# Combining five partial score maxima into the exponential's bias: from one VectorE instruction to three dependent GpSimd instructions

## The reference, cut to what matters

```python
attn = jnp.einsum('bhqd,bhkd->bhqk', q, k)          # q, k: integers of -127..127 times a step
attn = jax.nn.softmax(attn.astype(jnp.float32), axis=-1)
attn = _fq_unsigned(attn, axis=-1)                  # row maximum / 255 is the step; round to 0..255
out = jnp.einsum('bhqk,bhkd->bhqd', attn, v)
```

## Time and profile before

| | us |
|---|---|
| Three executions | 6569.11, 6581.19, 6591.67 |
| Median | 6581.19 |
| Profiled execution | 6572.37 |
| Its span, first to last instruction | 6570.9 |
| Cross-attention's unit stage, within the span | about 433 to 5330 |
| Busy within the span: VectorE | 5686.5 (87%) |
| ScalarE | 4572.5 (70%) |
| TensorE matmuls | 4523.2 (69%) |
| GpSimd | 4505.6 (69%) |

### The profile page before, as it was taken

The page is one execution under the profiler, slowest core; times in us unless marked ns, Lnnn a source line. Parts: engine busy times, 40 slices in busy tenths (PEclk is TensorE's granted clock), DMA queues, the critical chain, the costliest instruction groups (busy, mean ns, idle before and its releaser), DMA issues. The chain is left out here.

```text
span 6570.9 us, 141175 instructions
## 1 busy us (share of the span) xinstructions
PE 4523.2 (69%) x48970; PEld 2144.1 (33%) x49686; DVE 5686.5 (87%) x7938; ACT 4572.5 (70%) x4949; POOL 4505.6 (69%) x3196
## 2 busy tenths in 40 slices
PE   6736666666666666666666666666666645769999
PEld 3412222222222222222222222222222233454555
DVE  7579999999999999999999999999999955873222
ACT  3328888888888888888888888888888843331111
POOL 1238888888888888888888888888888833420000
PEclk9769999999999999999999999999999977989999
DMA  3137677677677677677777777766766740010000
GB/s 118 51 76 140 139 140 143 138 140 142 139 141 142 135 144 141 139 142 139 141 139 141 141 137 140 144 137 140 142 139 140 138 105 4 0 35 4 6 6 10
DMA packets 2231911, 735.21 MB, mean 112 GB/s; under 512 B 2175779, under 2 KB 2209412, under 8 KB 2225573
## 3 DMA queue, kind: packets, MB, share of 16 engines
q1 hardware_dynamic: 2196261, 576.08, 42.2%
q0 software_dynamic: 35456, 157.33, 13.2%
HBM read 168.97 MB, written 27.26 MB: 30 GB/s over the span
## 5 line engine op out<-in xcount | busy, mean ns | idle before, releaser
L803 DVE TENSOR_SCALAR_CACHE_REDUCE scores<-ring,step 128x2048 f32<-128x2048 f32 (+2 forms) x2560 | 4780.3, 1918 | 44.4 <-PE ring L730 28.0
L882 ACT ACTIVATE n_op<-scores,bias 128x2048 uint8<-128x2048 f32 x2048 | 4075.1, 1992 | 493.5 <-DVE m_rest L810 493.5
L678 POOL CAST nT<-pairs 128x2048 f16<-128x2048 uint8 x2048 | 3791.3, 1890 | 561.0 <-DMA pairs<-n_op 536.7
L730 PE MATMUL ring<-x_all,q_op 128*128 128x512 bf16 x7746 | 2153.7, 386 | 863.2 <-DVE scores L803 773.1
L730 PEld LDWEIGHTS ring<-x_all,q_op 128*128 128x128 bf16 x8192 | 683.0, 98 | 2021.1 <-DVE scores L803 1330.1
L727 PE MATMUL ring<-x_all,q_op 128*128 128x512 bf16 x1793 | 572.9, 390 | 808.0 <-DVE scores L803 780.3
L742 PE MATMUL pO<-nT,v_op 128*32 128x128 f16 x32768 | 660.1, 224 | 20.6 <-POOL nT L678 20.6
L742 PEld LDWEIGHTS pO<-nT,v_op 128*32 128x32 f16 x32768 | 478.5, 98 | 467.1 <-issue 359.2
L727 PEld LDWEIGHTS ring<-x_all,q_op 128*128 128x128 bf16 x2048 | 116.7, 97 | 1035.6 <-DVE scores L803 1028.3
L882 ACT ACTIVATION_READ_ACCUMULATOR n_op<-scores,bias 128x1 f32 x2048 | 384.7, 188 | 0.0
L1637 DVE TENSOR_TENSOR h_up<-h_gate,pUp 128x512 f32<-128x512 f32 x112 | 76.9, 687 | 298.2 <-ACT h_gate L1626 298.2
(11 more groups left out here) (194 smaller groups left out, 3293.2 us busy)
## 6 DMA issues: line engine op xcount, KB each, us to landing
x_all<-keys_transposed POOLq DMA_DIRECT2D x128, 768.0 KB, 8.4
v_st<-value_integers POOLq DMA_DIRECT2D x128, 256.0 KB, 3.5
pairs<-n_op SPq DMA_TRANSPOSE x2048, 2.8
keys_transposed<-kT_s POOLq DMA_DIRECT2D x32, 384.0 KB, 3.5
x_all<-in_x SPq DMA_DIRECT2D x2, 4096.0 KB, 14.9
cT<-in_ctx_T SPq DMA_DIRECT2D x32, 256.0 KB, 3.0
q_op<-queries_transposed POOLq DMA_DIRECT2D x384, 16.0 KB, 8.4
value_integers<-v_int SPq DMA_DIRECT2D x1, 4096.0 KB, 12.2
```

Source lines behind the costliest of these rows:

```text
L678: nc.gpsimd.tensor_copy(nT[par][:, j * EK:(j + 1) * EK, :].rearrange("p (a c) b -> p a c b", c=2), src).then_inc(s_un, 1)
L730: mm = nc.tensor.matmul(slot(t, j)[:, n * BANK:(n + 1) * BANK], q_op[b][:, t * P:(t + 1) * P], k_op[b][:, at + n * BANK:at + (n + 1) * BAN ...
L803: nc.vector.tensor_scalar(score[t % 2][:, at:at + width * BANK], slot(t, j)[:, 0:width * BANK], step[b][:, t:t + 1], None, ALU.mult, ALU.m ...
L882: nc.scalar.activation(n_op[par][:, j * EW:(j + 1) * EW], score[par][:, j * EW:(j + 1) * EW], ACT.Exp, bias=bias[par][:], scale=-1.0, accu ...
```

## The change

`make_bias` leaves VectorE's list and enters GpSimd's. There the five columns of `m_part` are combined in three instructions on one column each: min of columns 0, 1, 2; min of that with columns 3, 4; then ln 255 is added. The second and the third wait for the one before them on a new semaphore, `maxima_combined`. The bias of unit u+1 is made behind cast 0 of unit u (in unit 3 of a head group that is ahead of `keys`), and it waits for the last score copy, D4, of unit u+1. The bias of the first unit is made ahead of the loop.

```diff
@@ -533,7 +533,7 @@
         PAIRS = KT // 2
         HEADS = NG * H
         PE_STEPS = "M2 M3 AV0 M4 AV1 N0 N1 FOLD".split()
-        DVE_STEPS = "D0 BIAS FIN DEN D1 INV D2 D3 D4".split()
+        DVE_STEPS = "D0 FIN DEN D1 INV D2 D3 D4".split()
         ACT_STEPS = "E0 E1 OC E2 E3".split()
 
         assert NM % RING == 1 and all(sum(w) * BANK == NK for w in WIDTH)
@@ -569,6 +569,7 @@
         s_vo = sem("head_values_staged", xs)
         s_m = sem("scores_ready", xs)
         s_mu = sem("scores_copied", xs)
+        s_mr = sem("maxima_combined", xs)
         s_b = sem("bias_ready", xs)
         s_eu = sem("exp_done", xs)
         s_n = [[sem(f"turned{p}{j}", xs) for j in range(NE)] for p in range(2)]
@@ -678,10 +679,26 @@
                     nc.gpsimd.tensor_copy(nT[par][:, j * EK:(j + 1) * EK, :].rearrange("p (a c) b -> p a c b", c=2), src
                                           ).then_inc(s_un, 1)
 
+                def make_bias(u, par):
+                    pool.wait_ge(s_mu, scored(u, NM - 1))
+                    pool.sem_inc(s_turn, 1)
+                    m = m_part[par]
+                    nc.gpsimd.tensor_scalar(m_rest[par][:, 0:1], m[:, 0:1], m[:, 1:2], m[:, 2:3], ALU.min,
+                                            ALU.min).then_inc(s_mr, 1)
+                    pool.wait_ge(s_mr, u * 2 + 1)
+                    pool.sem_inc(s_turn, 1)
+                    nc.gpsimd.tensor_scalar(m_rest[par][:, 1:2], m_rest[par][:, 0:1], m[:, 3:4], m[:, 4:5], ALU.min,
+                                            ALU.min).then_inc(s_mr, 1)
+                    pool.wait_ge(s_mr, u * 2 + 2)
+                    pool.sem_inc(s_turn, 1)
+                    nc.gpsimd.tensor_scalar(bias[par][:], m_rest[par][:, 1:2], LN255, None, ALU.add).then_inc(s_b, 1)
+
                 def head(g, h, i):
                     for t in range(TG):
                         u = i * TG + t
                         unpack(u, t, 0)
+                        if exists(u + 1):
+                            make_bias(u + 1, (t + 1) % 2)
                         if t == 3 and exists(u + 2 * TG):
                             keys(g + (h + 2) // H, (h + 2) % H, i + 2)
                         unpack(u, t, 1)
@@ -708,6 +725,7 @@
                 for b in range(2):
                     pool.wait_ge(s_vo, b + 1)
                     load_values(2 + b, b)
+                make_bias(0, 0)
                 for h in range(H):
                     head(0, h, h)
                 with pool.Fori(1, NG - 1) as g:
@@ -804,12 +822,6 @@
                                             step[b][:, t:t + 1], None, ALU.mult, ALU.min,
                                             accum_out=m_part[t % 2][:, j:j + 1]).then_inc(s_mu, 1)
 
-                def make_bias(u, par):
-
-                    dve.wait_ge(s_mu, scored(u, NM - 1))
-                    nc.vector.tensor_scalar(m_rest[par][:], m_part[par][:], LN255, None, ALU.add, ALU.min,
-                                            accum_out=bias[par][:]).then_inc(s_b, 1)
-
                 def denominators(i, b):
                     dve.wait_ge(s_eu, exped(i * TG + TG - 1, NE - 1))
                     ge(dve, s_rd, i)
@@ -838,8 +850,6 @@
                                 if x == "D0" and t1 == 0:
                                     dve.wait_ge(s_st, i + 2)
                                 copy_scores(u + 1, int(x[1]), b, t1)
-                        elif x == "BIAS":
-                            make_bias(u, par)
                         elif t == 1 and exists(i - 1) and x != "FIN":
                             if x == "DEN":
                                 denominators(i - 1, 1 - hp)
```

## The result

The kernel after takes 7090.6 us in the median of four runs (7069.1 to 7092.2), against 6575.9 us for the kernel before beside it: ratio 1.078, 95% interval 1.076 to 1.080. The time of 7030 us was forecast, in a range of 6720 to 7400. The execution that the profiler recorded is the fastest of the four, 7069.1 us.

What follows compares the result with a forecast made beforehand. VectorE bounds before at 38.1 us per head group; then GpSimd at 33.7 + 4 x 0.96 + wait 4.1 = 41.6. The extra 3.5 x 128 = 450 us takes 6572 to 7022, plus 9 for the median: 7030, range 6720 to 7400.

Steps and rivals of the forecast that it cites:

- a wait of 2: GpSimd's wait for quarters behind the keys' load: 2 us instead of about 4 would show the prediction wrong.
- Its sign of over 3 us of idle time per head group at the score copies: VectorE's score copies: over 3 us idle per head group, put down to exponentials or TensorE, would show the prediction right.
- I take 0.18, by the COPY, which is nearest in size: Price of one new GpSimd instruction: 0.18 us, from a 4-element COPY; bounds 0.14 to 1.22.
- The wait of 0.23: GpSimd's new instructions: each wait for its own previous result costs 0.23 us, two per unit.
- b: GpSimd time added per unit by the three bias instructions: 2 x 0.18 + 2 x 0.23 + 0.14 = 0.96 us.
- So the transfer is issued 0.2 ahead of K: Unit 3's last quarter goes out 0.2 us before GpSimd issues the keys' load (8.3 against 8.5 after the bias).
- the long wait: GpSimd's wait per head group for a quarter sharing DMA engines with the keys' load: 4.1 us, used in the sum.
- up to 0.19 x 128 = 24 us more: VectorE ahead of FIN: extra saving of up to 24 us, if FIN's waits are taken during D0.
- 512 x 0.08 = 41: VectorE's saving from losing BIAS: 0.08 us each, 41 us in all, if VectorE stays the bound.
- Short wait: Rival: keys issued late enough for unit 3's last quarter to slip through; wait 2.1, round 39.6, time 6770; 16%.
- dearer instructions: Rival: GpSimd instructions with column operands have a fixed cost of 0.5 us; round 43.6 to 45.6, 7290 to 7540; 11%.
- GpSimd takes it in: Rival: GpSimd's round stays under 37.8 us, VectorE bounds and gives 41 to 65 us: 6516 to 6540; 9%.

Runs made afterwards that it cites:

- The chain beside the unchanged kernel: Kernel before, bias still on VectorE, plus the same three dependent GpSimd instructions at the same place on spare data, nobody waiting for them: 6827.9 us, ratio 1.038.
- the run without the dependence: Kernel after with three GpSimd instructions that read no result of each other, their two waits gone, bias constant: 7015.5 us, ratio 1.069.
- The run without a bias: Kernel before without any bias instruction; exponentials wait for their unit's last score copy and take a constant bias: 6522.9 us, ratio 0.992.
- the keys issued later: Kernel after with the keys' step in unit 3 moved behind cast 3 instead of behind the bias: 7134.7 us, ratio 1.086.
- five links: Kernel after with five dependent GpSimd instructions in place of three, two more copies of the second, same result: 7619.2 us, ratio 1.161.

## Why the prediction was right, and where two of its terms were not

**The bound.** Right: GpSimd's round of work plus its own wait took the lead over VectorE. Rounds foretold and measured: 41.6 and 42.0 us. The chain beside the unchanged kernel shows the work alone is enough for half of the loss. That the time came within 60 us is luck in part: two terms of the sum were wrong by over 200 us each, in opposite directions, and one of the prediction's own signs of being wrong, a wait of 2, did appear. Its sign of over 3 us of idle time per head group at the score copies did not: it was 116.0 / 47.7 = 2.4 us, with 101.3 / 47.7 = 2.1 more ahead of FIN.

**The price of the chain.** Mis-sized. "I take 0.18, by the COPY, which is nearest in size": two of the three take 0.36. They read two more operands from SBUF as columns. The third, with one constant, takes 0.22, and one with two operations on two constants takes 0.19 (the run without the dependence), so it is the columns and not the second operation that cost. The COPY was nearest in elements but not in operands; the TENSOR_SCALAR of rows 9 had the operands. The wait of 0.23 was right (0.21 and 0.20). The tail is 0.28 from the third instruction's start to the next and not 0.14, as nothing overlaps. b is 1.41 and not 0.96, which is 0.45 x 512 = 230 us too little. The rule of the Trainium skill (Perfetto Trace Analysis, "GPSIMD Engine Instruction"), to go by the spacing of starts, fits the three independent instructions: their spacings add up to 1.02 us (0.33, 0.44, 0.25) and their spans to 0.89. A spacing read where nothing waits is no price for dependent ones, though: the same instruction then has 0.57.

**The wait.** The step "So the transfer is issued 0.2 ahead of K" failed, and with it the long wait of 4.1: the wait is 1.9. The quarter goes out 0.96 us ahead of the keys. By the same formula, 0.45 more come from the chain, and 0.25 from the step copy, which takes 0.35 up to the keys' issue in place of 0.1 (3045.98 to 3046.33). The long wait was the right choice at 0.2 ahead, as 118 groups of before show. But I had read 1.95 as the nearest value with the short wait, and the same trace has it at 0.92. The wait was put at 2.2 x 128 = 280 us too much. The two errors have largely one root, the price of the chain, and opposite signs, and cancel to 50 us; the forecast is better than its terms.

**Smaller terms.** GpSimd's other work grew from 33.7 to about 34.4 us: `keys` from 2.09 to 2.49 (3004.03 to 3006.52), `values` from 2.21 to 2.30, casts from 1.84 to 1.85. These make up 0.7 x 128 = 90 us that were not foreseen; with them the balance is 230 - 280 + 90 = +40 us, of the 60 by which the forecast was too low (47 for the profiled execution, 7069 against the 7022 of the sum).

**VectorE's side.** The run without a bias gives 52 us, with an interval of 37 to 64, and the forecast of 41 to 65 holds as a number. As a sum, 512 x 0.08 = 41 has one BIAS in four too many, since the one ahead of FIN costs nothing: 384 x 0.08 = 31. Some 12 more can be put down to fewer idle copies (8.8 us in 2000 in place of 13.6); where the rest comes from stays open. The "up to 0.19 x 128 = 24 us more" was wrong: the gap ahead of FIN stays. The wait for D4 was indeed nothing: GpSimd's waits for score copies add up to 0.2 us in 2000.

**The rivals.** *Short wait* came true as to the wait, and with a b of 0.96 would have given 6770; *dearer instructions* came true in part (0.36 for two of three, under the 0.4 that it named). With only one of the two errors the miss would have been larger: 7260 with the true b and the long wait, 6770 with the short wait alone, 170 and 320 us off. *GpSimd takes it in* was false here, with one instruction too. It was true once 3.5 us of loads had left its list and the wait for quarters had come down to 1.6 us per group (86.5 us in 2000); there the advice of the Trainium skill (Perfetto Trace Analysis, "Optimizing Scalar/DVE Operations") to unload a saturated VectorE holds, for 0.3 to 0.5%.

## What to carry to other kernels

Before moving work to an engine that shows 69% busy, add up its list over one period of the stage, with the waits that it brings upon itself: here 33.7 us of work and 4.1 us of a wait hung on its own load stood against 38.1, and a chain that frees 0.08 us on VectorE cost 1.4 on GpSimd. Price a small instruction by a row with the same kinds of operands, not the same size, and a dependent one by the start-to-start distance of dependent ones. The wait behind a large load had two prices here, and less than half a microsecond in the order of issue decided which one was paid: a saving upstream can be eaten there. Before you choose between two such cases, sort all groups of the trace by that distance; two groups read one by one do not show where the switch lies.

## What was not expected of the hardware

- A GpSimd TENSOR_SCALAR on one element per partition takes 0.36 us with two column operands and 0.19 to 0.22 us with constants, so the two columns cost about 0.15 us.
- The issue of the keys takes 0.59 us in place of 0.51, and begins 0.35 us after the step copy in place of 0.12. The two have different conditions. The late start is there only with the dependent chain directly ahead of the step copy; with three independent instructions there, or a cast (the keys issued later), it is 0.13. The longer issue is there in each of these kernels, 0.58 behind a cast too, and 0.55 with a single instruction in each unit. What makes it longer no run shows.
- TensorE's granted clock in the stage is lower where the rounds are longer, 0.99 before, 0.92 after and 0.87 with five links (means of stretches at 2.4 GHz, which is 1, and at 1.2), and its 512-column score matmuls took 408 ns in place of 386. The windows from 500 to 5200 us of the three kernels, in this order (span, busy time and count of the five engines, granted clock, DMA share, GB/s):

```profile
500.00:5200.00 4700.00, 3138.78 (x41768) 1359.45 (x42445) 4655.59 (x6293) 4033.41 (x4072) 4105.21 (x2847) 0.99 0.71 140
```

```profile
500.00:5200.00 4700.00, 3192.45 (x38352) 1305.89 (x38352) 4190.11 (x4794) 3643.44 (x3678) 4169.60 (x3912) 0.92 0.64 127
```

```profile
500.00:5200.00 4700.00, 3048.18 (x34744) 1255.30 (x34732) 3825.65 (x4343) 3300.87 (x3334) 4076.56 (x4350) 0.87 0.58 115
```

In the kernel after, the clock falls to 1.2 GHz about once in each head group: 107 times from 700 to 5000 us, against 29 in before. Of these falls 91 come shortly behind an idle stretch of TensorE of over 2.5 us ahead of the fold matmul (L768), which waits for ScalarE's copy; before has no such stretch there. One of them, with the clock at 1.2 GHz from 3023.6 on:

```profile
3021.85 1.06 PE L768 MATMUL pO<-fold,oT 128*128 128x16 f32 x8 [3.03 <-ACT oT L899]
```

Whether the lower clock costs anything by itself in the kernel after was not tried; TensorE still waits for VectorE there (540.7 us ahead of L748), and the rounds come out by GpSimd's sums without it.
